# A transformer layer on one core: head groups in pairs in one accumulator bank, one transposition of the maxima, a shared buffer, and a new order

## The reference

```python
# x: (2, 1024, 128); 16 heads of 8; 16 experts of width 64, two shared ones
x = x + attn(layernorm(x))
x = x + ffn(layernorm(x))

def attn(x):
    q, k, v = (x @ W.T split into heads for W in (Wq, Wk, Wv))
    q, k = rope(layernorm(q) * q_gamma + q_beta), rope(layernorm(k) * k_gamma + k_beta)
    scores = where(causal, q @ k.T / sqrt(8), -inf)
    return softmax(scores) @ v, heads joined, @ Wo.T + bo

def ffn(x):
    p = softmax(x @ gate_w.T)                       # 16 experts in 4 groups
    combine = p on the two best experts of the two best groups (p + gate_b ranks them), else 0
    y = sum_e combine[e] * ((silu(x @ We1[e] + be1[e]) * (x @ We3[e] + be3[e])) @ We2[e] + be2[e])
    return y + (silu(x @ ws1 + bs1) * (x @ ws3 + bs3)) @ ws2 + bs2
```

## Time and profile before

| | |
|---|---|
| median of 3 runs (lowest, highest) | 418.56 us (415.84, 419.45) |
| span of the profiled execution | 414.9 us |
| chain that ended last | TensorE 45%, VectorE 35%, ScalarE 6%, DMA 3% of the span |
| largest groups | exponentials 141.0 us on ScalarE; reductions of maxima 95.7 + 75.6 us on VectorE; values products 77.4 us on TensorE |

### The profile page before, as it was taken

How to read it: one execution, slowest core, us unless ns; L and a number is a source line. 1 busy time by engine, 2 the same in 40 slices (tenths; PEclk the granted TensorE clock), 3 DMA queues, 4 the chain that set the end, 5 groups by cost and what they waited for, 6 DMA issues and landing times.

```text
span 414.9 us, 8178 instructions
## 1 busy us (share of the span) xinstructions
PE 352.3 (85%) x2999; PEld 153.8 (37%) x2999; DVE 314.9 (76%) x619; ACT 267.0 (64%) x395; POOL 151.3 (36%) x182
## 2 busy tenths in 40 slices
PE   2563388998989899999889999889887899999994
PEld 2332144554544343435223433224323242444431
DVE  4899998878899963789988977698998741265753
ACT  2543226775777874786782398767667689974850
POOL 0408967869401685001458100000000002664532
PEclk9865859999999999999999999999989999999999
DMA  3994004004100093300026000000000006300190
GB/s 95 223 181 128 24 16 139 5 2 116 43 3 1 3 207 75 104 2 0 1 73 135 28 2 3 2 2 1 2 2 4 2 2 130 78 0 0 30 202 25
DMA packets 26424, 21.69 MB, mean 52 GB/s; under 512 B 9201, under 2 KB 22162, under 8 KB 26322
## 3 DMA queue, kind: packets, MB, share of 16 engines
q1 hardware_dynamic: 24994, 20.12, 21.2%
q10 hardware_dynamic: 1392, 1.05, 1.0%
HBM read 13.56 MB, written 1.18 MB: 36 GB/s over the span
## 4 chain that ended last, share of the span: by engine, by line
PE 45%; DVE 35%; ACT 6%; issue 6%; DMA 3%; POOL 2%; SPq 2%; DVEq 0%; ACTq 0%; POOLq 0%
PE psum L687 14%; PE psum L666 8%; DVE mx_diag L1072 7%; DVE mx_full L1072 6%; PE psum L733 5%; PE psum L614 5%; PE psum L640 4%; PE psum L722 4%; ACT probs L795 4%; PE psum L596 4%; DVE mv L1144 2%; DVE nr L1012 2%; POOL mh L994 2%; DVE nr L1011 2%; DMA comb_b<-combine_scratch 2%
## 5 line engine op out<-in xcount | busy, mean ns | idle before, releaser
L795 ACT ACTIVATE probs<-psum 128x1024 f32<-128x1024 f32 x144 | 141.0, 1021 | 51.1 <-PE psum L614 29.9
L1072 DVE TENSOR_REDUCE mx_diag<-psum 128x4 f32<-128x512 f32 (+2 forms) x96 | 95.7, 1038 | 19.0 <-PE psum L640 17.9
L1072 DVE TENSOR_REDUCE mx_full<-psum 128x2 f32<-128x1024 f32 x64 | 75.6, 1217 | 16.9 <-PE psum L640 16.7
L994 POOL TENSOR_TENSOR mh<-mh,mv 128x512 f32<-128x512 f32 x36 | 45.2, 1269 | 93.0 <-DVE mv L1144 93.0
L687 PE MATMUL psum<-probs,v_ones 128*9 128x512 f32 (+3 forms) x768 | 77.4, 492 | 0.5 <-ACT probs L795 0.4
L722 PE MATMUL psum<-x2T,w 128*128 128x512 f32 x144 | 69.1, 606 | 1.5 <-ACT mv L832 0.8
L666 PE MATMUL psum<-q_st,k_st 64*128 64x512 bf16 (+3 forms) x384 | 53.8, 327 | 11.8 <-ACT probs L795 6.0
L640 PE MATMUL psum<-k_st,q_st 62*128 62x512 bf16 (+3 forms) x384 | 58.2, 337 | 4.1 <-ACT probs L795 2.5
L614 PE MATMUL psum<-masks 64*128 64x128 bf16 (+2 forms) x896 | 51.0, 213 | 11.8 <-DVE mx_diag L1072 9.2
L614 PEld LDWEIGHTS psum<-masks 64*128 64x128 bf16 x896 | 32.3, 95 | 45.6 <-DVE mx_diag L1072 23.2
L1144 DVE SCALAR_TENSOR_TENSOR mv<-psum,b,mv 128x512 f32<-128x512 f32 x36 | 26.3, 746 | 30.1 <-ACT mh L844 30.0
(11 more groups left out here) (146 smaller groups left out, 381.3 us busy)
## 6 DMA issues: line engine op xcount, KB each, us to landing
comb_b<-combine_scratch SPq DMA_DIRECT2D x32, 256.0 KB, 5.7
q_st<-parts SPq DMA_DIRECT2D x24, 128.0 KB, 2.3
k_st<-parts SPq DMA_DIRECT2D x18, 128.0 KB, 2.5
w<-in_We SPq DMA_DIRECT2D x3, 512.0 KB
k_st<-in_c_pad SPq DMA_DIRECT2D x2, 512.0 KB, 8.9
out<-xs SPq DMA_DIRECT2D x4, 256.0 KB, 2.3
xs<-in_x SPq DMA_DIRECT2D x3, 256.0 KB, 10.9
k_st<-parts ACTq DMA_DIRECT2D x6, 128.0 KB, 2.7
```

Of the source, the lines that this page charges most:

```text
L795: act.activation(probs[:, n % P_RING, :, :], wpair("scores", (s, i)), ACT.Exp, scale=SCALE).then_inc(exp_done, 1)
L994: pool.tensor_tensor(t, t, mv[:, at % V_RING, :], ALU.mult).then_inc(gate_done, 1)
L1072: dve.tensor_reduce(dst[:, a % 2, qt, :, pairs[0]:pairs[0] + nm], w, AX.X, ALU.max, negate=True).then_inc(max_free, 1)
```

## The change

1. **Two groups in one bank.** `v_ones` gets a row of nine zeros ahead of each head's nine columns. The stationary side of a values product is now 18 columns: of an even group its own nine, then zeros; of an odd group zeros, then its own nine. Even and odd group of a pair accumulate in one bank, only the even group's first product starts an accumulation, and `leave`, `oT`, `oT_read` run once for two groups: 8 of each. The rows of `Wo` are permuted on the host to the heads' new places. `ones` also writes the zeros.
2. **One transposition of the maxima.** `mx_full`, `mx_diag` and `negmax` have the four query tiles as their last index, so `mturn` is one transposition of 32 columns; `maxT` is 32 x 128 in the place of 8 x 512.
3. **Shared space.** `qk` and `sq` (early queries and keys) and `comb_b` now are one buffer, `early`. The first `cload` of chunk 0 also waits for `roped_ready` of all four chunks.
4. **A new order** of all stages, and new banks: fillings of one bank may now use banks 0 to 6.

```diff
-        qk = [sb(f"qk{i}", [P, TPC, 2, 2, HD, H // 2]) for i in range(2)]
-        sq = [sb(f"sq{i}", [P, TPC, 2, 2, H // 2, HD]) for i in range(2)]
+        early = sb("early", [P, 4, PAIRS // 4 * CH])
+        qk = [early[:, i, :].rearrange("p (t k a d m) -> p t k a d m", t=TPC, k=2, a=2, d=HD) for i in range(2)]
+        sq = [early[:, 2 + i, :].rearrange("p (t k a m d) -> p t k a m d", t=TPC, k=2, a=2, d=HD) for i in range(2)]
...
-        v_ones = sb("v_ones", [P, B, KT, H, VC])
+        v_ones = sb("v_ones", [P, B, KT, H + 1, 2, VC])
...
-        comb_b = sb("comb_b", [P, PAIRS, CH])
+        comb_b = early[:, :, :].rearrange("p a (u q) -> p (a u) q", q=CH)
...
-                    if x >= 1:
+                    if x == 0:
+                        sp.wait_ge(roped_ready, NX)
+                    else:
...
-                for qt in range(TPC):
-                    src = negmax[:, qt, :, :, :].rearrange("p a r m -> p (a r m)")
-                    last = pe.transpose(wb[0:8, qt * P:(qt + 1) * P], src, ident_bf[:, :])
-                last.then_inc(work_full, 1)
+                src = negmax[:, :, :, :, :].rearrange("p a r m t -> p (a r m t)")
+                pe.transpose(w.bitcast(BF16)[0:8 * TPC, 0:P], src, ident_bf[:, :]).then_inc(work_full, 1)
...
-                if k == 0 and a >= 1:
-                    pe.wait_ge(o_ready, a)
+                if k == 0 and a >= 2 and g % 2 == 0:
+                    pe.wait_ge(o_ready, a // 2)
...
-                    last = pe.matmul(acc[32 * j:32 * j + VC, q0:q0 + cols], v_ones[:, b, kt, G * g + j, :],
-                                     probs[:, n % P_RING, j % 2, col:col + cols], start=(kt == 0),
-                                     stop=(k == len(bursts_of(c)) - 1), tile_position=(0, 32 * j),
+                    at = 2 * VC * (G * g + j) + VC * (1 - g % 2)
+                    own_then_zeros = v_ones[:, b, kt, :, :, :].rearrange("p h z v -> p (h z v)")[:, at:at + 2 * VC]
+                    last = pe.matmul(acc[32 * j:32 * j + 2 * VC, q0:q0 + cols], own_then_zeros,
+                                     probs[:, n % P_RING, j % 2, col:col + cols], start=(kt == 0 and g % 2 == 0),
+                                     stop=(k == len(bursts_of(c)) - 1 and g % 2 == 1), tile_position=(0, 32 * j),
                                      skip_group_check=True)
...
-                    pool.memset(v_ones[:, arg, :, :, HD:VC], 1.0).then_inc(v_set, 1)
+                    pool.memset(v_ones[:, arg, :, :, 0, :], 0.0)
+                    pool.memset(v_ones[:, arg, :, :, 1, HD:VC], 1.0).then_inc(v_set, 1)
...
+    given["Wo"] = given["Wo"].reshape(D, NG, G, HD).transpose(0, 2, 1, 3).reshape(D, D)
```

289 lines of the change are left out of this document (142 added, 147 removed).

## The result

The changed kernel takes 390.32 us (median of 4 runs, 388.1 to 396.79) where the kernel before, run on the same chip, takes 417.2. The ratio is 0.9347, 95% interval 0.9287 to 0.9406: 6.5% faster, 26.9 us. The prediction said 404 with a range from 394 to 416: the right side, 14 us too little, and outside the range.

The account below looks back on a forecast made before the run. The prediction took TensorE's work to bound 60 to 260 us. Head 5, middle 8.5 and tail 1 made 14.5 us off 414.9, so 400.4; adding 3.7 from span to median gave 404.1, range 394 to 416.

Parts of the forecast that it names:

- head: Kernel start: new VectorE order brings the first reduction to 41.5 from 50.17 us; gain 5 us, bounds 0 and 9.5.
- middle: Between head and tail: 10.2 us of removed TensorE work gives 8.5 us, bounds 4 and 10.2.
- tail: After the last copy of o_raw: earlier gate products save about 1.3 us; net gain 1 us, bounds -2 and 2.
- What bounds the kernel: From 60 to 260 us TensorE is busy 187.4 of 200 us, so its work is the time there.
- the order moves the nine output products: In the middle, moving chunk 0's expert output products and spreading chunk 1's into TensorE's idle stretch was given nothing.
- this is in the counts: Accumulator emptied once per pair: the next group's wait for the copy is halved, with no separate gain in the sum.
- Rival (a): From 260 to 340 us the new order also takes up half of TensorE's 12.0 us idle: 398 us, chance 0.15.
- (b): Whole kernel: less work, no less time, VectorE keeps the pace, half of the middle stays: 414 us, chance 0.16.
- (c): Expert products of chunk 0 fall behind on GpSimd, twice 10 us: 424 us, chance 0.11; sign: GpSimd releasing moe_y.
- (d): No savings: wider stationary side costs 3.8 us, mrow 8; 416 us, chance 0.08; sign: a load above 95 ns.
- The stationary side: Weight loads of values products: 18 columns for 9 cost nothing; upper end 5 ns on each of 768, 3.8 us.
- VectorE and ScalarE, part 1 and 2: Instruction times: product 0.42 us, reciprocal 0.27, copy to maxT 0.278; ScalarE's 9.3 and VectorE's 3.2 us not counted again.

Follow-up runs that it names:

- e1: Parts 1 to 3 of the change in the order and banks of before, without the odd groups' separate turns: 414.73 us, ratio 0.9915 to the kernel before.
- a_y0_block: Changed kernel with eight expert output products of chunk 0 in one block behind pv.25, GpSimd's work for them moved up: 402.24 us, ratio 0.9645.
- a_y1_block: Changed kernel with six expert output products of chunk 1 in one block behind pv.35, GpSimd's work for them moved up: 395.85 us, ratio 0.9494.
- a_x2_late: Changed kernel with the first six expert products of chunk 2 moved behind mrow.15, after the last maximum: 401.34 us, ratio 0.9622.
- e10: Changed kernel, order kept, banks moved so that 123 of 160 maximum tiles use banks 4 and 5: 463.91 us, ratio 1.1091.
- e6: New structure, order of before up to the first score tile, new order behind it: 398.8 us, ratio 0.9526.
- a_extra_copy: Changed kernel with an added ScalarE copy of the accumulator after each even group, for which the odd group's first values product waits: 395.51 us, ratio 0.9485.
- a_headsum_again: Changed kernel with headsum.1 ahead of norm.2 on VectorE and rstd_pool.1 ahead of the lower parts on GpSimd, as before: 397.26 us, ratio 0.9495.
- e5: New structure, new order up to the first score tile, order of before behind it: 417.75 us, ratio 1.0021.
- e13: New structure, new order kept up to scores.6.0, order of before behind it: 418.7 us, ratio 1.003.
- a_four_mturns: Changed kernel with part 2 undone, four transpositions of the maxima and the 8 x 512 copy again: 393.14 us, ratio 0.9425.

## Why the prediction was right and wrong

Its sum was 14.5 us against 26.5: head 5 for 11.3, middle 8.5 for 17.0, tail 1 for −1.8, which makes the 12.0 between them (6.3 + 8.5 − 2.8). In the middle's sum there is a small slip: 10.2 − 7.1 leaves 3.1 beyond 260 us, not 2.9. The other 1.9 us is the distance from span to median, 3.7 added from a single execution before: it is 1.8 here (390.17 and a span of 388.4).

**What bounds the kernel: wrong for the order of before.** "From 60 to 260 us TensorE is busy 187.4 of 200 us: there its work is the time." By this e1, with the removed work gone, should have given the 8.5 us of the middle; it gave 3.5, 2 to 5 by its interval. Our reading is that a busy share of 94% with 6% of waits, most of them on the reader of a pair of banks, is a loop of TensorE, VectorE and ScalarE, in which work removed from one member lengthens its waits; the rows of e1 fit this. The rows that could have warned are the idle columns by line (L666: 11.8, L640: 4.1) and the chain, at 45% TensorE; the prediction read neither. In the changed kernel the number for this stretch came out, 7.1 us up to 260 forecast and 8.8 measured between the first and the 65th exp, 7.8 of it busy time. That is in part luck, since by e1 the same work in the old order gives less than half.

**The middle, 8.5 for 17.0.** The count of the removed work was right: 32 turns of o_raw, 16 of the maxima at 230 ns, busy time 11.6 us lower (10.2 counted). What failed is "the order moves the nine output products ... I give it nothing": this term was put at 0, and 8.2 us of idle time went in the middle, 7.2 of them behind the 65th exp. The blocks of a_y0_block, a_y1_block and a_x2_late cost 6 to 14 us each, and the bank pairs of e10 75; from the old rest to the new one, with the structure new and the head old, it is 16 us (e1 to e6). The accumulator's hand-over, "this is in the counts", was not: 5 to 7 us (a_extra_copy). The failed step is thus to price the parts one by one, with the order at nothing: parts 1 and 2 alone give 0.85%, the order alone 0.7%, both 6.5%.

**The head, 5 for 11.3.** The mechanism was right in its detail: first reduction 39.97 for a forecast of 41.5, first scores 58.5 for 60, norm.3 no longer beside a long product, and the two moves alone worth 6.7 us (a_headsum_again). The size was not: 3.6 us were taken off for qkv.12 to 15, and the 5.9 left were taken as 5 without a row; 9.5 was the upper bound. The lead does fall from 11.3 to 7.0 at the 19th exp, but it is 10.7 again at the 31st, and by e6 9 us of it are kept to the end. But this too holds only with the new rest: e5 and e13 keep nothing.

**Rival (a), idle time between 260 and 340 taken up: it happened.** By equal work it is 7.2 us behind the 65th exp, for 6 us with a chance of 0.15. It was right in kind and nearly in size, and stood alone, at 398; the outcome needs it and the head in full. The "one accumulator wait in two" named for it is borne out by a_extra_copy, which is level with the changed kernel at the 65th exp and 5.5 us behind at the last copy of o_raw. (b), less work and no less time, is what the structure does in the old order (e1), so it was a good rival to have and the order is what refutes it. (c), the experts late on GpSimd, shows in small: its sign, GpSimd as the releaser of the output products, is there (2.7 of 3.5 us of waits, before the change 0.8 of 3.7), but for 1 us in the pattern of chunk 1 and not 10, and for 2.8 us in the first profiled execution; a_y0_block shows that the place of these products matters, at the predicted size of some 10 us, by another mechanism. (d) did not happen, although its sign did, as follows.

**The stationary side.** "A load of 9 takes 89 ns and one of 16 also 89 ns, so I take nothing."

```profile
L685 PEld LDWEIGHTS psum<-probs,v_ones 128*18 128x18 f32 x768 | 15.9, 97 | 25.4 <-issue 22.2 <-ACT probs L793 2.0
```

It is 97 ns for 18 columns, 8 ns more for each than before, above the upper end of 5; as many loads overlap, their busy time grew by 2.4 us only. The Trainium skill's rule (TensorE: Matmul & The Clock Gate, What happens when you issue a matmul) gave 7.5 ns and was near the measured step, though not for 9 and 16 columns, which take the same. The prediction said that a load above 95 ns makes (d); that sign was wrong, for nothing of the cost shows: the values products' own time fell from 77.4 to 76.1 us and TensorE stands idle 0.2 us before them.

**VectorE and ScalarE, part 1 and 2.** The product of twice the width takes 424 ns (0.42 taken), the reciprocal 352 (0.27 taken), the copy to maxT 248 (0.278 taken), a memset of the zeros 1.2 us (0.35 to 3.5 taken). mrow's pieces of 256 bytes cost nothing that shows; a_four_mturns, without them, is slower.

**The tail** is 55.7 us from the last copy of o_raw, for 53 forecast and 53.9 before: the saving of 1.3 us is not there, and no run was spent on the 1.8.

**Chances.** Forecast and rivals were made as alternatives, each with one mechanism. The likeliest case held neither a gain by order in the middle nor an interaction. Rival (a) with the head at its upper bound, 9.5 for 5, would have been 398 − 4.5 = 393.5, just below the range, which left it out as two cases at once; the measured time is still 3 us below.

## What to carry to other kernels

A stretch in which the leading engine is busy 94% need not be bound by that engine's work: read what the 6% wait for, by line, and the leading engine's share of the chain; where the waits are for the readers of its own output buffers, removed work can turn into waits until the buffers are dealt and the filler work spread anew. Compare two profiles between the same pieces of work, and not between the same times. Where a change comes with an order made for it, price the pair, not the parts: an order fits one set of durations, and half of a new one can be slower than either whole. Do not let two tiles with a slow reader follow each other in one buffer, do not stand chained units in a block, and count the hand-over of a shared accumulator as a wait of its own.
